# Empty places of the sorted edge tables: gathered as row 0, or left out of the gather by a bound

## The chip, the cores and the metric

One Trainium2 chip, one of its cores. The time is the device time of one execution in microseconds. The kernel before ran three times: 5455.31 us median, 5442.81 lowest, 5456.56 highest.

## The reference

A graph of 3125 nodes with 256 features goes through four residual layers, each behind a layer norm. Two of the four hold the attention over edges that this case is about:

```python
x = x + L0_gnn(...)   # sum over 50000 edges of weight * (x @ W)[src], into dst
x = x + L0_ffn(...)   # 32768 edges + one loop per node: attention with 16 features, 4 heads;
                      # it gives gates over 4 experts, then the experts
x = x + L1_gnn(...)   # three layers of _gat_conv over 50000 edges + one loop per node
x = x + L1_ffn(...)   # routing to 2 of 8 experts

def _gat_conv(x, src, dst, W, a_src, a_dst, b, n_nodes):      # 4 heads x 64 features
    h = (x @ W).reshape(n_nodes, Hh, Cc)
    e = leaky_relu(e_src[src] + e_dst[dst], 0.2)
    m = segment_max(e, dst); ex = exp(e - m[dst])
    alpha = ex / (segment_sum(ex, dst)[dst] + 1e-16)
    out = segment_sum(h[src] * alpha[:, :, None], dst)
    return out.reshape(n_nodes, Hh * Cc) + b
```

The sources of the edges are drawn evenly over the nodes. The targets of the 50000 edges crowd at the low nodes (3125 * u^2 for an even u). The outputs are the 3125 x 256 features.

## The kernel before

The program is a row of stages. A stage is one block in which every engine runs its own list of instructions, with semaphores between them; between two stages all engines meet at a barrier (L1709). There is no planner: the order on an engine is the order in which the code is written.

**Sorting.** The edges are sorted by target once, on the chip. A sorted table has columns of 128 places, one place per partition. Targets are grouped in buckets of 32 nodes, and a bucket starts a column of its own, so its last column is filled up with empty places; whole columns behind the last bucket are empty too, up to a multiple of 24. The table of the 50000 edges has room for 504 columns (`NCF`), that of the 32768 edges for 360 (`NCFG`). `permute_edges` (L408) brings the records of the 50000-edge table to their places with matmuls on one-hot matrices; `sum_edges` (L747) does the same for the 32768-edge table beside its own work. Both end with a few VectorE instructions that unpack the result: `whole` >> 2 is the place's node in its bucket plus one (zero at an empty place), `lows` becomes a penalty that the attention subtracts, and `sources` (`rows` in `permute_edges`) is the row of the source node. At an empty place it is 0, so an empty place reads row 0, and the penalty takes it out of the sum.

**Attention.** `attend_edges` (L846) runs in four stages: once on the 32768-edge table with rows of 24 numbers (`table_gate`, 96 bytes), and three times on the 50000-edge table with rows of 264 numbers (`table_att`, 1056 bytes). A group is 4 columns (`QD`); a ring of 6 slots (`U`) holds gathered rows, and one trip of the loop goes once around the ring.

- GpSimd (POOL) issues four indirect DMAs for each group (L892), each for one column, 128 rows. Before them it waits for the indices (`staged`, copied by ScalarE in L993) and, from the second trip on, until the slot has been used (`summed`).
- For each group VectorE waits until the slot's four DMAs have landed (`landed`), and subtracts the penalty (L911). TensorE transposes (L1056), VectorE takes the maximum (L942) and the running maximum, ScalarE and VectorE form the weights (L1007, L932, L1017), TensorE transposes back (L1064), ScalarE copies (L1024), and TensorE multiplies weights and rows (L1072). VectorE adds them to the bucket (L926).
- On VectorE, L911 of group q+1 stands ahead of L942 of group q.

At the start of such a stage SyncE loads the attention terms and the self loops' rows (L878, L880), and VectorE clears and copies a few small tables (L966 to L973).

Of the kernel before, what the change touches and what calls it, by code (L numbers as in the profile page):

```python
# [5 lines left out]
P = 128  # L6
# [4 lines left out]
NT = (N + P - 1) // P  # L11
# [15 lines left out]
ABOVE = 65536.0  # L27
RANKS = 4

ALU = mybir.AluOpType  # L30
# [18 lines left out]
NCFG = columns_sorted(EG)  # L49
# [358 lines left out]
def permute_edges(nc, block, m, name, edges, nch, record, lows, rows):  # L408
# [10 lines left out]
    def _(dve):  # L419
# [13 lines left out]
        whole, part = m.work[:, 13200:13200 + ncol].bitcast(I32), m.work[:, 13200 + ncol:13200 + 2 * ncol].bitcast(I32)  # L433
        chain.next(nc.vector.tensor_copy(whole, ps[0]))
# [3 lines left out]
        chain.next(nc.vector.scalar_tensor_tensor(rows, part, 1024.0, ps[1], ALU.mult, ALU.add))  # L438
# [301 lines left out]
def sum_edges(nc, block, m, name, table, rec, index, bucket, bias_in, edges, nch, record, lows, sources):  # L740
# [24 lines left out]
    def _(dve):  # L765
# [18 lines left out]
        def unpack():  # L784
            chain = Chain(dve, steps)
            dve.wait_ge(moved, fc)
            whole, part = m.sums.whole[:, 0:nch].bitcast(I32), m.sums.part[:, 0:nch].bitcast(I32)
            chain.next(nc.vector.tensor_copy(whole, ps_moved[0]))
            nc.vector.tensor_scalar(part, whole, 3, None, ALU.bitwise_and)
            chain.next(nc.vector.tensor_scalar(whole, whole, 2, None, ALU.logical_shift_right))  # L790
            nc.vector.tensor_scalar(lows, whole, -1.0, -STEP, ALU.add, ALU.mult)
            chain.next(nc.vector.scalar_tensor_tensor(sources, part, 1024.0, ps_moved[1], ALU.mult, ALU.add))
# [54 lines left out]
def attend_edges(nc, block, m, name, width, table, at_dram, nch, lows, rows_in, bucket, own_hot, starts, trip_count):  # L847
# [8 lines left out]
    s_ = lambda n: m.sem(f"{name}_{n}")  # L856
    passed, staged, fenced, masked, turned, reduced, lifted, leaked, top, exped, shrunk, turned2, evacd, summed, taken, steps, acc_in, at_in, tabled, ready = (
# [26 lines left out]
    def _(pool):  # L884
        def gather(q, s, first=False):
            pool.wait_ge(staged, q + 1)
            pool.sem_inc(passed, 1)
            if not first:
                pool.wait_ge(summed, q + (1 - U))
                pool.sem_inc(passed, 1)  # L890
            for t in range(QD):
                nc.gpsimd.indirect_dma_start(  # L892
                    out=rows[s][:, t, :], out_offset=None, in_=table[:, 0:rw],
                    in_offset=bass.IndirectOffsetOnAxis(ap=f.index[s][:, t:t + 1], axis=0)).then_inc(landed[s], 16)
# [9 lines left out]
    def _(dve):  # L904
# [60 lines left out]

        nc.vector.memset(running[:, 0:1], 0.0)  # L966
# [594 lines left out]
def memory(nc, ctx):  # L1561
# [91 lines left out]
    f.whole, f.part = view(NCFG), view(NCFG)  # L1653
# [160 lines left out]
```

## Time and profile before

| | |
|---|---|
| median of three runs | 5455.31 us |
| profiled execution, from the first instruction to the last (its span) | 4248.4 us |
| median less span | 1206.9 us |
| columns gathered in the four attention stages | 288, 456, 456, 456 |
| POOL busy | 2415.2 us (57%) |
| DVE busy (VectorE) | 2892.6 us (68%) |
| ACT busy (ScalarE) | 2269.8 us (53%) |
| PE busy (TensorE) | 2975.2 us (70%) |
| rows read by POOL's queue | 245.97 MB, 23.0% of the DMA engines' span |

The trace holds one profiled execution. It gives the span and no time of that execution outside it; the timed runs are longer than the span by 1206.9 us, for which there are no rows. All times of instructions below count from the first instruction of the span. A busy POOL is one that builds the descriptors of a gather; the transfer itself is not in that time.

### The profile page before, as it was taken

To read this page: it belongs to the slowest core of one execution; us is meant where nothing else is said; L and a number is where in the kernel's file an instruction comes from. 1 tells how busy PE (TensorE), PEld (TensorE's weight loads), DVE (VectorE), ACT (ScalarE), POOL (GpSimd) and SP (SyncE) were. 2 spreads that over 40 slices of the span, in tenths; PEclk is the share of its full clock that TensorE was granted. 3 is DMA by queue.
4 is the path that set the end of the run, shared out by engine and by line. 5 is a ranking of instruction groups with operands and counts; after the bars stand their busy time and mean duration, and the time that the engine had idled before them with its cause. 6 is when DMAs were issued, how large, how long until landed. Compare 5 with 4: busy or idle time off the path is not lost. (4 is left out here: it accounts for less than half of the span.)

```text
span 4248.4 us, 90006 instructions
## 1 busy us (share of the span) xinstructions
PE 2975.2 (70%) x23535; PEld 1861.8 (44%) x23535; DVE 2892.6 (68%) x9698; ACT 2269.8 (53%) x7978; POOL 2415.2 (57%) x2556
## 2 busy tenths in 40 slices
PE   5488957776666649997676666577666677766188
PEld 4252223333333337775344444344443444444166
DVE  6769977777447772224687777588777588777715
ACT  2006933333257762112687774487776388777423
POOL 3777767777357750000777773577775477777010
PEclk8558989999655559998555556655555755555599
DMA  2000023333210010001644442544443534444000
GB/s 97 6 2 2 2 78 105 106 106 105 46 14 10 10 30 12 12 0 43 138 108 108 108 108 60 125 108 108 108 108 84 113 109 108 108 108 102 3 23 30
DMA packets 199883, 292.96 MB, mean 69 GB/s; under 512 B 110324, under 2 KB 139998, under 8 KB 199678
## 3 DMA queue, kind: packets, MB, share of 16 engines
q0 software_dynamic: 108400, 245.97, 23.0%
q1 hardware_dynamic: 91310, 44.97, 4.4%
q8 instruction: 74, 1.21, 0.1%
q14 instruction: 99, 0.81, 0.1%
HBM read 270.29 MB, written 20.48 MB: 68 GB/s over the span
## 5 line engine op out<-in xcount | busy, mean ns | idle before, releaser
L892 POOL DMA_INDIRECT work<-table_att,work x1368 | 1297.2, 948 | 917.7 <-ACT work L993 500.7
L1064 PE MATMUL psum<-ident,work 128*128 128x128 f32 x1656 | 558.8, 474 | 362.1 <-ACT work L1017 362.1
L1017 ACT ACTIVATE work<-work 128x128 f32<-128x128 f32 x1656 | 529.6, 390 | 236.3 <-DVE work L932 236.3
L1072 PE MATMUL psum<-work 128*32 128x65 f32 (+1 forms) x13248 | 418.4, 294 | 314.1 <-ACT work L1024 261.8
L1064 PEld LDWEIGHTS psum<-ident,work 128*128 128x128 f32 x1656 | 301.3, 182 | 663.2 <-ACT work L1017 489.5
L1072 PEld LDWEIGHTS psum<-work 128*32 128x32 f32 x13248 | 331.3, 164 | 433.7 <-DVE acc L926 369.7
L932 DVE SCALAR_TENSOR_TENSOR work<-psum,work 128x128 f32<-128x128 f32 x1656 | 465.0, 343 | 82.2 <-ACT work L1007 77.3
L1007 ACT ACTIVATE work<-psum,work 128x128 f32<-128x128 f32 x1656 | 475.2, 375 | 49.7 <-DVE work L942 48.9
L926 DVE SCALAR_TENSOR_TENSOR acc<-acc,work,psum 128x65 f32 (+1 forms) x1656 | 445.5, 269 | 77.3 <-DMA acc<-table_att 16.6
L1056 PE MATMUL psum<-ident,work 128*128 128x128 f32 x1656 | 461.9, 435 | 36.2 <-DVE work L911 35.1
L474 POOL DMA_INDIRECT sorted<-xt x392 | 388.4, 991 | 171.3 <-issue 119.6
L817 POOL DMA_INDIRECT work<-table_sum,index x415 | 399.9, 964 | 142.0 <-PE psum L842 96.6
L911 DVE TENSOR_TENSOR work<-work,psum 128x512 f32<-128x512 f32 x414 | 283.8, 685 | 275.0 <-issue 168.3
L842 PE MATMUL psum<-work 128*128 128x256 f32 x830 | 289.0, 436 | 178.7 <-DMA work<-table_sum,index 107.0
L1000 ACT ACTIVATE psum<-iota,lows 128x32 f32<-128x32 f32 x1656 | 393.4, 311 | 31.3 <-DVE work L973 31.3
L892 POOL DMA_INDIRECT work<-table_gate,work x288 | 272.4, 946 | 181.8 <-ACT work L993 94.3
L1024 ACT COPY work<-psum 128x512 f32<-128x512 f32 x414 | 243.0, 587 | 198.6 <-PE psum L1064 198.6
L1056 PEld LDWEIGHTS psum<-ident,work 128*128 128x128 f32 x1656 | 296.3, 217 | 103.2 <-issue 59.4
L1414 PE MATMUL psum<-xt,work 128*128 (+1 forms) x960 | 267.8, 437 | 53.6 <-DMA work<-in_L_ffn_b_dram,expert_rows 35.3
L826 ACT ACTIVATE work<-work,xn 128x128 f16<-128x128 f16 x256 | 102.8, 401 | 358.1 <-DVE work L782 358.0
L942 DVE TENSOR_REDUCE work<-psum 128x512 f32 (+1 forms) x414 | 285.5, 690 | 3.1 <-issue 0.3
L1455 ACT ACTIVATE work<-psum,work 128x640 f32<-128x640 f32 x120 | 95.3, 794 | 342.6 <-PE psum L1414 342.5
(310 smaller groups left out, 4592.9 us busy)
## 6 DMA issues: line engine op xcount, KB each, us to landing
work<-table_att,work POOLq DMA_INDIRECT x1368
table_att<-acc SPq DMA_DIRECT2D x75, 132.0 KB
acc<-table_att SPq DMA_DIRECT2D x12, 812.5 KB
work<-table_sum,index POOLq DMA_INDIRECT x415, 2.7
sorted<-xt POOLq DMA_INDIRECT x392, 2.1
work<-table_gate,work POOLq DMA_INDIRECT x288, 2.3
work<-in_L_ffn_W_dram SPq DMA_DIRECT2D x8, 512.0 KB, 4.8
table_sum<-acc SPq DMA_DIRECT2D x25, 128.0 KB
```

Source lines behind the costliest of these rows:

```text
L474: nc.gpsimd.indirect_dma_start(out=rec_dram[s], out_offset=bass.IndirectOffsetOnAxis(ap=row[:, f:f + 1], axis=0), in_=record[:, f, :], in_ ...
L817: nc.gpsimd.indirect_dma_start(out=f.rows[c % RS][:, :], out_offset=None, in_=table, in_offset=bass.IndirectOffsetOnAxis(ap=index[:, c:c + ...
L842: nc.tensor.matmul(ps[c % PS], f.hot[c % PS][:, :], f.rows[c % RS][:, :], start=True, stop=True).then_inc(summed, 1)
L892: nc.gpsimd.indirect_dma_start(out=rows[s][:, t, :], out_offset=None, in_=table[:, 0:rw], in_offset=bass.IndirectOffsetOnAxis(ap=f.index[s ...
L926: nc.vector.scalar_tensor_tensor(acc[:, b, :], acc[:, b, :], f.fac[s][:, t:t + 1], ps_s[s % 2][:, t, :], ALU.mult, ALU.add).then_inc(taken, 1)
L932: ins = nc.vector.scalar_tensor_tensor(fifth, ps_z[s % 2][:, t * P:(t + 1) * P], dst[:, bass.ds(q * QD + t, 1)], fifth, ALU.add, ALU.max)
L1000: ins = nc.scalar.activation(ps_pen[s % 2][:, t, :], m.iota[:, 0:DB], ACT.Square, scale=STEP, bias=lows[:, bass.ds(q * QD + t, 1)])
L1007: ins = nc.scalar.activation(f.y[s % 2][:, t, :], ps_z[s % 2][:, t * P:(t + 1) * P], ACT.Identity, scale=0.2, bias=fifth_dst[:, bass.ds(q ...
L1017: nc.scalar.activation(f.pt[s % 2][:, t, :], f.y[s % 2][:, t, :], ACT.Exp, bias=f.neg[s][:, t, 1:2]).then_inc(exped, 1)
L1056: ins = nc.tensor.transpose(ps_z[s % 2][:, t * P:(t + 1) * P], f.z[s % 2][:, t, :, :].rearrange("p h d -> p (h d)"), m.ident[:, :])
L1064: nc.tensor.transpose(ps_p[s % 2][:, t * P:(t + 1) * P], f.pt[s % 2][:, t, :], m.ident[:, :]).then_inc(turned2, 1)
L1072: ins = nc.tensor.matmul(ps_s[s % 2][DB * h:DB * (h + 1), t, :], f.p[s % 2][:, t, DB * h:DB * (h + 1)], rows[s][:, t, h * w1:(h + 1) * w1] ...
```

## The change

At an empty place `sources` becomes 65536 + 0 in place of 0 (`NOWHERE`), worked out by two more VectorE instructions in each of the two unpackings. The gathers of the attention get a bound, the last row of the table (3199), and rows beyond it are left out without an error: nothing is written to their place in the slot. Since a place in a slot could then hold anything at first, VectorE sets the six slots to zero at the start of each attention stage, and the first gather into a slot waits for that (`cleared`). The gathers of `sum_edges` (L817) and the scatters of the sort (L474) are as before.

```diff
--- before.py
+++ after.py
@@ -25,6 +25,7 @@
 LN_EPS = 1e-5
 BIG = 1e30
 ABOVE = 65536.0
+NOWHERE = 65536.0
 RANKS = 4
 
 ALU = mybir.AluOpType
@@ -431,11 +432,14 @@
                                     ALU.is_equal, ALU.mult).then_inc(built, 1)
         dve.wait_ge(moved, fc)
         whole, part = m.work[:, 13200:13200 + ncol].bitcast(I32), m.work[:, 13200 + ncol:13200 + 2 * ncol].bitcast(I32)
+        nowhere = m.work[:, 13200 + 2 * ncol:13200 + 3 * ncol]
         chain.next(nc.vector.tensor_copy(whole, ps[0]))
         nc.vector.tensor_scalar(part, whole, 3, None, ALU.bitwise_and)
         chain.next(nc.vector.tensor_scalar(whole, whole, 2, None, ALU.logical_shift_right))
         nc.vector.tensor_scalar(lows, whole, -1.0, -STEP, ALU.add, ALU.mult)
-        chain.next(nc.vector.scalar_tensor_tensor(rows, part, 1024.0, ps[1], ALU.mult, ALU.add))
+        chain.next(nc.vector.tensor_scalar(nowhere, whole, 0.0, NOWHERE, ALU.is_equal, ALU.mult))
+        chain.next(nc.vector.scalar_tensor_tensor(nowhere, part, 1024.0, nowhere, ALU.mult, ALU.add))
+        chain.next(nc.vector.tensor_tensor(rows, nowhere, ps[1], ALU.add))
 
     @block.scalar
     def _(act):
@@ -789,7 +793,10 @@
             nc.vector.tensor_scalar(part, whole, 3, None, ALU.bitwise_and)
             chain.next(nc.vector.tensor_scalar(whole, whole, 2, None, ALU.logical_shift_right))
             nc.vector.tensor_scalar(lows, whole, -1.0, -STEP, ALU.add, ALU.mult)
-            chain.next(nc.vector.scalar_tensor_tensor(sources, part, 1024.0, ps_moved[1], ALU.mult, ALU.add))
+            nowhere = m.sums.nowhere[:, 0:nch]
+            chain.next(nc.vector.tensor_scalar(nowhere, whole, 0.0, NOWHERE, ALU.is_equal, ALU.mult))
+            chain.next(nc.vector.scalar_tensor_tensor(nowhere, part, 1024.0, nowhere, ALU.mult, ALU.add))
+            chain.next(nc.vector.tensor_tensor(sources, nowhere, ps_moved[1], ALU.add))
 
         for c in range(PS):
             mark(c)
@@ -854,6 +861,7 @@
     rw = hw + HEADS
     U = GROUP // QD
     s_ = lambda n: m.sem(f"{name}_{n}")
+    cleared = m.sem(f"{name}_cleared")
     passed, staged, fenced, masked, turned, reduced, lifted, leaked, top, exped, shrunk, turned2, evacd, summed, taken, steps, acc_in, at_in, tabled, ready = (
         s_(n) for n in ("passed", "staged", "fenced", "masked", "turned", "reduced", "lifted", "leaked", "top", "exped", "shrunk", "turned2", "evacd", "summed", "taken", "steps",
                         "accin", "atin", "tabled", "ready"))
@@ -885,13 +893,16 @@
         def gather(q, s, first=False):
             pool.wait_ge(staged, q + 1)
             pool.sem_inc(passed, 1)
-            if not first:
+            if first:
+                pool.wait_ge(cleared, s + 1)
+            else:
                 pool.wait_ge(summed, q + (1 - U))
                 pool.sem_inc(passed, 1)
             for t in range(QD):
                 nc.gpsimd.indirect_dma_start(
                     out=rows[s][:, t, :], out_offset=None, in_=table[:, 0:rw],
-                    in_offset=bass.IndirectOffsetOnAxis(ap=f.index[s][:, t:t + 1], axis=0)).then_inc(landed[s], 16)
+                    in_offset=bass.IndirectOffsetOnAxis(ap=f.index[s][:, t:t + 1], axis=0),
+                    bounds_check=NT * P - 1, oob_is_err=False).then_inc(landed[s], 16)
 
         trips = pool.value_load(trip_count, min_val=least, max_val=most)
         for k in range(U):
@@ -963,6 +974,8 @@
             nc.vector.tensor_tensor(f.drop[k], neg[:, :, 1], neg[:, :, 0], ALU.subtract).then_inc(top, 1)
             leak(q, k)
 
+        for s in range(U):
+            nc.vector.memset(rows[s], 0.0).then_inc(cleared, 1)
         nc.vector.memset(running[:, 0:1], 0.0)
         odd = reset.rearrange("p (c k) -> p c k", k=2)
         nc.vector.memset(odd[:, :, 1], 0.0)
@@ -1650,7 +1663,7 @@
     f = m.sums = Memory()
     f.rows = [view(D) for _ in range(16)]
     f.hot = [view(P) for _ in range(6)]
-    f.whole, f.part = view(NCFG), view(NCFG)
+    f.whole, f.part, f.nowhere = view(NCFG), view(NCFG), view(NCFG)
     assert at[0] <= WORK, at[0]
     at[0] = 0
     f = m.flash = Memory()
```

On VectorE, in the unpacking of the 50000-edge table (`permute_edges`; `sources` is what the diff calls `rows`), before:

```order
L434 CAST work<-psum 128x504
L435 TENSOR_SCALAR work<-work 128x504
L436 TENSOR_SCALAR work<-work 128x504
L437 TENSOR_SCALAR lows<-work 128x504
L438 SCALAR_TENSOR_TENSOR sources<-work,psum 128x504
```

and now:

```order
L436 CAST work<-psum 128x504
L437 TENSOR_SCALAR work<-work 128x504
L438 TENSOR_SCALAR work<-work 128x504
L439 TENSOR_SCALAR lows<-work 128x504
L440 TENSOR_SCALAR work<-work 128x504
L441 SCALAR_TENSOR_TENSOR work<-work 128x504
L442 TENSOR_TENSOR sources<-work,psum 128x504
```

The one instruction that formed `sources` has become three; the next one on the engine is the first of `merge_edges`. The unpacking in `sum_edges` grows in the same way, with 360 columns.

On VectorE, at the start of an attention stage with rows of 264 numbers, before:

```order
L966 MEMSET work 128x1
L968 MEMSET work 128x504
L969 COPY work<-starts 128x504
L971 COPY work<-psum 128x504
L972 COPY work<-psum 128x504
```

and now:

```order
L978 MEMSET work 128x1056 x6
L979 MEMSET work 128x1
L981 MEMSET work 128x504
L982 COPY work<-starts 128x504
L984 COPY work<-psum 128x504
L985 COPY work<-psum 128x504
```

Six clearings of 128 x 1056 numbers stand ahead of the stage's first instruction; in the stage with rows of 24 numbers they are 128 x 4 x 24 each. Nothing else is moved, and POOL issues the same instructions in the same order, 4 gathers for a group.

## Rows read from the trace of the kernel before

**Rows 1.** The page, its first line.

```profile
span 4248.4 us, 90006 instructions
```

**Rows 2.** Windows, gate attention stage and first of the three others; last PEclk, DMA, GB/s.

```profile
1198.50:1558.40 359.90, 212.32 (x2771) 138.29 (x2772) 260.99 (x973) 275.69 (x1047) 272.37 (x288) 0.50 0.12 11
2015.70:2586.70 571.00, 391.45 (x4416) 256.56 (x4416) 439.38 (x1552) 438.04 (x1671) 432.30 (x456) 0.50 0.46 114
```

**Rows 3.** L892, first of the three: ns min/median/max, first and last start.

```profile
L892 POOL DMA_INDIRECT work<-table_att,work x456: 945/949/958, 2015.7 to 2585.7; - x152
```

**Rows 4.** Timeline within that stage: start, us, engine, line, [idle <-releaser].

```profile
2403.86 0.69 DVE L942 TENSOR_REDUCE work<-psum 128x512 f32 x1
...
2405.38 0.95 POOL L892 DMA_INDIRECT work<-table_att,work  x1 [0.30 <-issue]
...
2408.22 0.69 DVE L911 TENSOR_TENSOR work<-work,psum 128x512 f32<-128x512 f32 x1 [0.81 <-issue]
...
2408.86 0.69 DVE L942 TENSOR_REDUCE work<-psum 128x512 f32 x1
```

**Rows 5.** Timeline, DVE, early in the third stage.

```profile
3444.08 0.68 DVE L942 TENSOR_REDUCE work<-psum 128x512 f32 x1
...
3448.83 0.68 DVE L942 TENSOR_REDUCE work<-psum 128x512 f32 x1
```

**Rows 6.** Timeline, end of the first of the three stages.

```profile
2585.73 0.95 POOL L892 DMA_INDIRECT work<-table_att,work  x1 [0.30 <-issue]
...
2592.49 0.69 DVE L911 TENSOR_TENSOR work<-work,psum 128x512 f32<-128x512 f32 x1 [2.41 <-issue]
...
2596.95 0.68 DVE L942 TENSOR_REDUCE work<-psum 128x512 f32 x1
```

**Rows 7.** Timeline, ends of the other two and of the gate stage.

```profile
3260.04 0.95 POOL L892 DMA_INDIRECT work<-table_att,work  x1 [0.30 <-issue]
...
3266.75 0.69 DVE L911 TENSOR_TENSOR work<-work,psum 128x512 f32<-128x512 f32 x1 [2.31 <-issue]
...
3921.25 0.95 POOL L892 DMA_INDIRECT work<-table_att,work  x1 [0.30 <-issue]
...
3928.31 0.69 DVE L911 TENSOR_TENSOR work<-work,psum 128x512 f32<-128x512 f32 x1 [2.72 <-issue]
...
1557.47 0.95 POOL L892 DMA_INDIRECT work<-table_gate,work  x1 [0.30 <-issue]
...
1560.80 0.69 DVE L911 TENSOR_TENSOR work<-work,psum 128x512 f32<-128x512 f32 x1 [1.48 <-issue]
```

**Rows 8.** DMA queues, 2300 to 2320 us: packets, MB, share of 16 engines.

```profile
q0 software_dynamic: 771, 2.16, 39.6%
```

**Rows 9.** DMA queues, 2575 to 2590 us.

```profile
q0 software_dynamic: 456, 1.31, 76.6%
```

**Rows 10.** Timeline, start of the first of the three stages.

```profile
2014.40 0.67 ACT L993 COPY work<-sources 128x4 int32<-128x4 int32 x6 [5.29 <-PEq L1709]
...
2014.60 0.48 DVE L968 MEMSET work<- 128x504 f32 x1
...
2015.71 0.95 POOL L892 DMA_INDIRECT work<-table_att,work  x1 [457.29 <-ACT work L993]
...
2026.70 0.69 DVE L911 TENSOR_TENSOR work<-work,psum 128x512 f32<-128x512 f32 x1 [3.54 <-DMA work<-table_att,work]
...
2031.70 0.68 DVE L942 TENSOR_REDUCE work<-psum 128x4 f32<-128x512 f32 x1
```

**Rows 11.** Timeline, DVE, unpacking in permute_edges and what follows.

```profile
556.84 0.67 DVE L438 SCALAR_TENSOR_TENSOR sources<-work,psum 128x504 int32<-128x504 int32 x1
571.61 1.46 DVE L498 TENSOR_TENSOR work<-work 128x1245 f32<-128x1245 f32 x1 [14.10 <-DMA work<-sorted]
```

**Rows 12.** Groups of instructions, DVE, x in sum_edges: busy, mean ns, idle before.

```profile
L775 DVE TENSOR_TENSOR x<-x,psum 128x256 f32 x415 | 174.3, 420 | 127.7 <-PE psum L842 123.0 <-DVE x L797 0.8 <-DVE sources L792 0.6
```

**Rows 13.** L474, the scatters of the sort: duration ns min/median/max.

```profile
L474 POOL DMA_INDIRECT sorted<-xt x392: 955/962/3138, 53.3 to 561.4; - x196
```

## The prediction

> **What bounds the kernel now.** I read the page first: the span is 4248.4 us [rows 1], while the timed median is 5455.3. The 1206.9 us between them have no rows. I take them as the same before and after, so the sum is made against the span and its result is carried over to the median microsecond for microsecond.
>
> Next the windows of the four attention stages. The reader is to see POOL's count: 288 gathers in 359.9 us, 456 in 571.0 us [rows 2], so 1.25 us each. POOL's busy share is 76%, but the rest is no slack: one gather takes 949 ns, between 945 and 958 over all 456 [rows 3], and 0.30 us of issue stands before each [rows 4]. POOL never stops for anything else, so the stage is as long as POOL's list: 456 x 1.25 = 571 us. The other two stages with 1056-byte rows also have 456 gathers; together 3 x 571 + 360 = 2073 us of the span go by POOL's issue rate.
>
> The timeline shows the distance of the second limit. In the middle of a stage two maxima (L942, one for each group) start 5.00 us apart, four gathers of 1.25 [rows 4]. Early in a stage, where the engines still work off what POOL had fetched ahead, they start 4.75 us apart [rows 5]: that is the compute chain's own pace, only 0.25 us under POOL's. The 0.50 of PEclk in those windows [rows 2] is the 1.2 GHz level, after stretches in which PE was busy 60 to 70% of the time. It is in the 4.75 already.
>
> The third thing is what lies behind the last gather. In the middle, L911 starts 2.84 us after its group's fourth gather started [rows 4]. For the last group of a stage that is 6.76 us [rows 6], 6.71 and 7.06 in the other two [rows 7], and 3.33 in the gate stage with its 96-byte rows [rows 7]. The last columns are empty, and all 128 rows of such a gather are row 0. The DMA rows say the same: 2.16 MB took 39.6% of 20 us [rows 8], 1.31 MB near the end took 76.6% of 15 us [rows 9]. Per MB that is 3.7 against 8.8 us of the queue. Many reads of one row are slow here; in the middle this hides behind POOL, at the end it does not.
>
> **The change part by part.**
>
> *Rows left out.* The 50000-edge table has 456 x 128 = 58368 gathered places, 8368 of them empty (14.3%). The gate table has 36864, with 4096 empty (11.1%). Those rows are no longer transferred. In the middle this is worth nothing: the transfers use 40% of the queue and POOL sets the pace. At the ends the lags should come back to the 2.84 us of the middle: 6.76 - 2.84 = 3.9, then 3.9 and 4.2, together 12.0 us. In the gate stage 0.5 us may go; I count nothing. Behind L911 comes a chain of fixed work, which moves with it: the group before it could start its maximum no sooner than 4.75 us after the one before, and the middle's spacing leaves that room.
>
> *The bound itself, on POOL.* No row shows a gather with a bound. POOL issues as many instructions as before, so the question is only whether 949 ns stays. Its price is multiplied by 1656 and nothing hides it, since POOL is the bound. From below: if all of a gather's time belonged to its rows, 14.3% fewer of them would take 136 ns off. From above: if each row were gone through twice, once for the bound, 949 ns would come on top. The nearest row for a gather's sister with other addressing is the scatter, 962 ns against 949 [rows 13, 3], so 13 ns apart, 22 us over all. The durations do not move with bytes either, so I take zero, and keep both ends for the rivals.
>
> *The clearing.* Six memsets of 1056 numbers at the start of a stage. One of 504 numbers takes 0.48 us [rows 10], so 1.0 us each, 6.0 us in all (six of 0.1 us in the gate stage). VectorE has room for more than half of it in the 3.54 us that it waited for the first landing before L911 [rows 10]. The rest fits into the 12.1 us from its first instructions at 2014.6 to L911 at 2026.70, which hold six instructions on 504 numbers or fewer, some 0.5 us each by the memset's row. The new wait on POOL stands ahead of the first gather of each slot, and the whole ring is queued behind it. The first slot is clear about 1.0 us into the stage, at 2015.5; POOL started at 2015.71 [rows 10]. The other slots come 5 us apart and are clear long before. If POOL needs after this semaphore what it needed after ScalarE's copy (2014.5 to 2015.7), its start moves by 1 us; if not, by nothing. Half of it, three times: +1.5 us. If the cover were gone altogether, it would be 3 x 6 = 18 us.
>
> *Two more instructions in each unpacking.* At most 0.67 us each for 504 numbers [rows 11]. In the first, VectorE then waits 14.10 us for a DMA [rows 11]: hidden. In `sum_edges` VectorE waits for TensorE 123 us in all before its additions [rows 12]; the 0.9 us there are made up over the last twelve columns: zero.
>
> *Sum.* -12.0 + 1.5 = -10.5 us. On the span 4248.4 - 10.5 = 4237.9, on the median 5455.3 - 10.5 = 5444.8.
>
> By the Trainium skill (DMA: Bandwidth & Descriptors, Anatomy of one DMA — SWDGE (gpsimd) path) a software DMA takes 2.0 us plus its bytes over 436 GB/s, whichever rows it reads; the lag at the end would then have another cause and would stay, and the sum would be +1.5 us, 5456.8. The trace speaks against that rule here, since gathers of equal size lag 2.84 and 6.76 us; this is the last rival below.
>
> **The rivals.**
>
> *POOL gets faster.* Fewer rows may mean less work for POOL. For it speaks that 949 ns for 128 rows is 7.4 ns a row, which looks like work by row; against it that the duration never varies, so that nothing shows a share by row. With 136 ns less, four gathers take 4 x 1.118 = 4.47 us, under the compute chain's 4.75. Then compute is the bound: from the first L942 at 2031.70 [rows 10], 113 steps of 4.75 end at 2568.5, where the last L942 was at 2596.95 [rows 6], 28.5 us less. The gate stage has 71 steps of 0.25, 17.8 us. Together 3 x 28.5 + 17.8 = 103, less some 5 us a stage, an estimate from the slow first landings (the 3.54 us wait), plus the 1.5: -87 us, 5368. The end effect is in it. The share needed by row is small: 63 ns less already reach 4.75.
>
> The Trainium skill (the same page, SWDGE vs HWDGE vs iDMA) has a Q7 core compute one descriptor pair for each DMA operation, which would make POOL's time go by the rows that are left, and give this rival's 5368. No row here shows a gather with fewer than 128 rows.
>
> *The bound costs POOL time (the other side).* The place is L892, each of its 1656 gathers. The price is any time for comparing and leaving out, paid in full because POOL never rests in these stages; from 6 ns a gather on (10.5 us / 1656) the change is no gain, from 16 ns on it is slower by over 0.3%. For it speaks that a row's 7.4 ns leave little room for a branch; against it the 13 ns between gather and scatter, which already differ in what is addressed. A tenth of a row's time more, 0.74 ns x 128 = 95 ns, makes 157 us: 5455.3 - 10.5 + 157 = 5602. A second pass would be 1572 us, which I hold very unlikely.
>
> *The ends do not shorten.* The bound may be applied without taking the load away, for instance if left-out rows still go through the queue, or the lag is that of the ring's last entries and not of row 0. Then only the clearing is left: +1.5 us, 5457. Against it speaks the queue's time per MB [rows 8, 9].
>
> **How the numbers follow.** Forecast (POOL unchanged, ends shorter) 0.47; POOL faster 0.14; the bound costs 0.33; ends unchanged 0.06. The predicted time is that of the forecast, 5445, with a range of its own of 5435 to 5457. The whole range runs from the faster rival, 5365, into the dear one as far as a price of 142 ns a gather (+235 us), 5680; beyond it I leave about 0.12, and below 0.03. A change of 0.3% is 16.4 us, about what a measurement of this kernel tells from none. The forecast's -10.5 lies inside it, but its parts can reach beyond: 0.16 of its 0.47 go to faster, 0.31 to the same. With the others: faster 0.14 + 0.16 = 0.30; same 0.31 + 0.06 and 0.02 for a bound of a few ns = 0.39; slower 0.31.
>
> **What would show it.** The first number to read is the mean of the attention gathers on POOL: 949 ns if right; under 900 the first rival, over 960 the second. L942 should stay 5.00 us apart in the middle; at 4.75 compute has become the bound. The lag from the last group's fourth gather to L911 should be under 3.2 us in all three stages. The queue's time per MB should be the same at the end as in the middle. POOL's first gather of a stage should start within 1 us of where it did. L498 should still wait about 13 us for its DMA. The prediction is wrong if the gathers' duration or their 0.30 us spacing has moved, or if the median moves and the span does not, since the 1206.9 us were only assumed to stay.

## The result: 0.6 to 0.8% slower, in a kernel with two paces

The changed kernel took 5485.42 us (median of 4 runs, 5474.84 to 5497.84) against 5455.73 (4 runs): 1.0063 times as long, 95% interval 1.0047 to 1.0079. The forecast was 5445 (5435 to 5457): the wrong direction, outside the forecast's own range and inside the whole one of 5365 to 5680. Ratios leave out one run, a 5813.08 us of e13 below, at a granted clock of 0.549 where its eleven others had 0.617 to 0.626. The profiled execution took 5474.84 us, and its page begins:

```profile
span 5473.1 us, 91690 instructions
```

Span and time agree here, unlike [rows 1], where 4248.4 us stood for a kernel timed at 5455. A profile of the unchanged kernel taken beside timed runs (experiment e1) explains it:

```profile
span 5446.1 us, 90006 instructions
```

The trace that the prediction read was of an execution unlike the timed ones. In five later series the same unchanged kernel took 5448, 4243, 5486, 5447 and 4246 us; the first two were on one and the same chip. I call this the quick and the slow pace; the instructions are the same in both, and nothing here shows what switches it. Its mark is in the second stage, where POOL issues scatters back to back beside the projection. The copies of the projection's tiles (L628) follow each other at 1.08 us in the quick trace:

```profile
85.98 0.37 ACT L628 COPY work<-psum 128x256 f32<-128x256 f32 x1 [0.71 <-PE psum L643]
87.07 0.37 ACT L628 COPY work<-psum 128x256 f32<-128x256 f32 x1 [0.71 <-PE psum L643]
```

and at 16.8 us in e1, where the second of these copies starts 13.9 us after TensorE's last transposes (L643) ended:

```profile
218.06 0.37 ACT L628 COPY work<-psum 128x256 f32<-128x256 f32 x1 [16.44 <-remote]
...
220.35 0.63 PE L643 MATMUL psum<-ident,xn 128*128 128x128 f32 x2
...
234.85 0.37 ACT L628 COPY work<-psum 128x256 f32<-128x256 f32 x1 [16.42 <-remote]
```

In the slow pace TensorE's signals are held back while POOL issues indirect DMAs. Work beside which POOL issues none is as fast in both paces: the copies of the projection ahead of the gate attention run from 1129.3 to 1190.3 us in the quick trace and from 1660.3 to 1721.3 in e1, 61.0 us in both. The stages with indirect DMAs lose 1.2 ms together. TensorE itself is not slower there: in the first wide attention stage (rows of 264 numbers) the granted clock is 0.50, the 1.2 GHz level, in both traces, and one of its transposes back (L1064) takes 476 ns in both. An attention stage in e1 looks like this (before, slow pace):

```profile
3022.71 0.69 DVE L942 TENSOR_REDUCE work<-psum 128x512 f32 x1 [2.43 <-remote]
3023.28 0.94 POOL L892 DMA_INDIRECT work<-table_att,work  x1 [1.87 <-remote]
...
3026.84 1.35 PE L1064 MATMUL psum<-ident,work 128*128 128x128 f32 x4 [1.26 <-ACT work L1017]
3027.03 0.95 POOL L892 DMA_INDIRECT work<-table_att,work  x1 [0.30 <-issue]
3029.33 0.69 DVE L942 TENSOR_REDUCE work<-psum 128x512 f32 x1 [2.47 <-remote]
```

Groups are 6.62 us apart, not the 5.00 of [rows 4], and POOL, which "never stops" in the quick trace, waits 1.9 us ahead of a group. L942 waits until 3029.33 for the transposes of L1056, whose last had ended at 3025.57. The trace's semaphore events tell that it is the signals that are late: six of TensorE arrive between 3029.11 and 3029.31, those of L1072 and L1056, whose last matmuls had ended 4.6 and 3.6 us before (the profile models matmul ends), and all four of L1064, and one of POOL's own between them, at 3029.16. In the quick trace the four of L1064 come 0.3 us apart. Now the changed kernel in the same place:

```profile
3022.95 0.69 DVE L953 TENSOR_REDUCE work<-psum 128x512 f32 x1 [5.00 <-DMA att<-in_L_ffn_att_dst_dram]
...
3023.59 1.00 POOL L902 DMA_INDIRECT work<-table_att,work  x1 [2.19 <-remote]
...
3026.46 0.67 DVE L922 TENSOR_TENSOR work<-work,psum 128x512 f32<-128x512 f32 x1
3027.11 1.35 PE L1077 MATMUL psum<-ident,work 128*128 128x128 f32 x4 [1.30 <-ACT work L1030]
3027.50 1.00 POOL L902 DMA_INDIRECT work<-table_att,work  x1 [0.30 <-issue]
...
3029.67 0.69 DVE L953 TENSOR_REDUCE work<-psum 128x512 f32 x1 [2.54 <-DMA att<-in_L_ffn_att_dst_dram]
```

The group is 6.72 us; the median of all is 6.70 against 6.61 (L911, L942 and L892 are now L922, L953 and L902). The load that the profile names ahead of L953 was done over a millisecond before; L953 waits for the same signal as L942 above. What answers to [rows 3] is the gather's own time, with a second row that before does not have:

```profile
L902 POOLq MOVE  x1656: 29/29/38, 1722.0 to 5135.3; - x184
L902 POOL DMA_INDIRECT work<-table_att,work x1368: 992/998/1218, 2666.0 to 5138.4; - x196
```

A gather with a bound takes 998 ns instead of 949, and POOL's queue moves the bound's value into a register ahead of each (29 ns). The page's DMA row, after and then e1:

```profile
q0 software_dynamic: 108400, 219.18, 15.5%
```

```profile
q0 software_dynamic: 108400, 245.97, 18.3%
```

27 MB fewer, but not one packet fewer. A gather makes 32 packets of four rows (4224 bytes) and 16 small ones; where rows are left out, the sizes in the trace are 3172, 2120, 1068 and 16 bytes, so a row left out leaves 4 bytes in a packet that is still there.

The end of the first wide stage, after, answers to [rows 6]:

```profile
3424.00 1.00 POOL L902 DMA_INDIRECT work<-table_att,work  x1 [0.31 <-issue]
...
3434.34 0.68 DVE L922 TENSOR_TENSOR work<-work,psum 128x512 f32<-128x512 f32 x1
```

and e1 in the same place:

```profile
3411.46 0.95 POOL L892 DMA_INDIRECT work<-table_att,work  x1 [0.30 <-issue]
...
3421.98 0.68 DVE L911 TENSOR_TENSOR work<-work,psum 128x512 f32<-128x512 f32 x1
```

10.3 us against 10.5, with nothing of DMA in the idle time: in the slow pace L911 of the last two groups still lies ahead when the last gather starts, the rows have landed before their turn, and nothing can be won there. The queue did become faster at the end, as forecast. From 3400 to 3430 us, after and then e1:

```profile
q0 software_dynamic: 768, 0.83, 11.1%
```

```profile
q0 software_dynamic: 426, 1.19, 33.7%
```

That is 4.0 us of the queue per MB against 8.5, where [rows 8] gave 3.7 for the middle. Packets of 4224 bytes that start between 3410 and 3420 us in the changed kernel, with four real rows each, take 0.17 us (median); e1's behind 3412 us, with row 0 four times, take 0.75. So row 0 is the cause of the slow end, not the place in the ring.

The start answers to [rows 10]:

```profile
2664.04 0.67 ACT L1006 COPY work<-sources 128x4 int32<-128x4 int32 x6 [5.29 <-PEq L1722]
...
2664.32 0.94 DVE L978 MEMSET work<- 128x1056 f32 x1 [4.26 <-PEq L1722]
...
2666.05 0.99 POOL L902 DMA_INDIRECT work<-table_att,work  x1 [467.25 <-DVE work L978]
```

Memsets of 0.94 us, and POOL's first gather 2.01 us after ScalarE's copies instead of 1.31.

### The profile page after: what moved, and what is told of

Same layout as the page of the kernel before. It is cut to its first block and busy times, and to the rows that moved or that the text cites. A ratio compares the mean times of both kernels' runs of the same rounds, so it can differ in the third digit from the quotient of the medians.

```text
span 5473.1 us, 91690 instructions
## 1 busy us (share of the span) xinstructions
PE 3002.8 (55%) x23535; PEld 1936.2 (35%) x23535; DVE 2848.4 (52%) x9726; ACT 2294.2 (42%) x7978; POOL 2512.4 (46%) x2556
## 3 DMA queue, kind: packets, MB, share of 16 engines
q0 software_dynamic: 108400, 219.18, 15.5%
## 5 line engine op out<-in xcount | busy, mean ns | idle before, releaser
L902 POOL DMA_INDIRECT work<-table_att,work x1368 | 1364.7, 998 | 1420.8 <-remote 567.4
L953 DVE TENSOR_REDUCE work<-psum 128x512 f32 (+1 forms) x414 | 285.9, 691 | 1019.5 <-DMA att<-in_L_ffn_att_dst_dram 835.5
L478 POOL DMA_INDIRECT sorted<-xt x392 | 402.2, 1026 | 169.8 <-issue 119.5
L902 POOL DMA_INDIRECT work<-table_gate,work x288 | 286.8, 996 | 288.9 <-remote 116.0
L670 PE MATMUL psum<-work 128*128 128x260 f32 (+1 forms) x400 | 140.5, 482 | 302.5 <-issue 203.6
L922 DVE TENSOR_TENSOR work<-work,psum 128x512 f32<-128x512 f32 x414 | 280.2, 677 | 50.2 <-DMA work<-table_att,work 24.4
L779 DVE TENSOR_TENSOR x<-x,psum 128x256 f32 x415 | 173.4, 418 | 237.3 <-PE psum L849 144.1
```

The source lines that it names most:

```text
L478: nc.gpsimd.indirect_dma_start(out=rec_dram[s], out_offset=bass.IndirectOffsetOnAxis(ap=row[:, f:f + 1], axis=0), in_=record[:, f, :], in_ ...
L902: nc.gpsimd.indirect_dma_start(out=rows[s][:, t, :], out_offset=None, in_=table[:, 0:rw], in_offset=bass.IndirectOffsetOnAxis(ap=f.index[s ...
```

## The experiments

Times are medians, ratios are against the unchanged kernel on the same chip, with 95% intervals. Which pace a series would meet couldn't be chosen.

### The change in its parts (e1 to e4, slow pace, before at 5447.9 us)

e1 is the kernel before. e2 has the bound alone:

```diff
-                    in_offset=bass.IndirectOffsetOnAxis(ap=f.index[s][:, t:t + 1], axis=0)).then_inc(landed[s], 16)
+                    in_offset=bass.IndirectOffsetOnAxis(ap=f.index[s][:, t:t + 1], axis=0),
+                    bounds_check=NT * P - 1, oob_is_err=False).then_inc(landed[s], 16)
```

e3 has everything but the bound (`NOWHERE = 0.0`, no `bounds_check`), and e4 is the changed kernel.

> The kernel before, unchanged, profiled once more. The trace read for the prediction has a span of 4248 us where the timed runs take 5455; the changed kernel's span (5473 us) and its time (5475 us) agree. Theory 1 (held signals, whatever the kernel): in the timed executions of both kernels TensorE's semaphore signals are held back while POOL issues gathers without a pause; the span here is then about 5454 us, with maxima (in the attention loop) some 6.5 us apart (4 gathers of 1.25 and 1.5 us of pause) in place of 5.0, and gathers of 949 ns. Theory 2 (the change brought the held signals): the span here is 4250 us again, maxima 5.0 us apart, and 1200 us still lie outside it.

> Only the bound on the attention gathers; empty places still read row 0, no clearing, so no row is left out. Theory 1 (the bound has a price on POOL, whatever it leaves out): the gathers take 998 ns in place of 949, and the time is +30 to +83 us (1656 x 0.05). Theory 2 (the price lies in leaving rows out, or in the clearing): gathers of 949 ns, 0 +- 5 us.

> Only the clearing of the six slots with the wait of the first gathers, and the three instructions of each unpacking with the added row number set to 0; no bound, empty places read row 0. Theory 1 (the bound is the price): gathers of 949 ns, +1 to +4 us for a later first gather. Theory 2 (the clearing costs, since POOL's queue stands behind it at four stage starts): +10 to +30 us.

> The changed kernel unchanged, timed in the same rounds as its parts. Theory 1: +30 us (5485), the sum of a price of the bound (+83 at most) and a gain of the rows left out (about -50). Theory 2 (the first measurement was a matter of the chip): within 0.3% of before.

Measured: e1 5448.97 (1.0002); e2 5477.21 us (1.0055, 1.0042 to 1.0069); e3 5454.08 (1.0011, 1.0002 to 1.0020); e4 5484.56 (1.0071, 1.0057 to 1.0084). The parts, 29.3 + 6.2 = 35.5 us, make the whole, 36.7: the bound costs, and the rows left out are worth nothing (e4's expectation had given them 50 us). Clearing moves the four attention stages of e3 by about 1 us in all; the rest of its 6 us (1 to 11 by the interval) lies mostly in the second stage, which took 965 to 984 us over thirteen slow profiles of all these kernels. Gathers are 998 ns in e2, where no row is left out, as in e4, where 14% are.

### Quick pace (e5 to e8, before at 4242.6 us)

e5 lets every place of the attention tables point beyond the bound (`ALU.is_equal` to `ALU.is_ge` in both unpackings), and so leaves out rows that the result needs. e6 has no bound but a memset behind each fourth gather:

```diff
+            if not isinstance(q, int) or q:
+                pool.wait_ge(padded, q)
+                pool.sem_inc(passed, 1)
+            nc.gpsimd.memset(m.prod[:, 0, 0:P], 0.0).then_inc(padded, 1)
```

e7 has the bound where `t < 2` alone. e8 pauses the scatters of the second stage:

```diff
             if f >= COPIES:
                 pool.wait_ge(sent[s], 16 * (f // COPIES))
+            if f >= COPIES and s == 0:
+                pool.wait_ge(sent[COPIES - 1], 16 * (f // COPIES))
```

> Leaves out all rows that the attention stages gather: every place of their tables, not the empty ones alone, points beyond the bound, so that no row of 1056 bytes is brought in those stages. Theory 'the price of the bound is paid once per gather on POOL, whatever its rows': gathers still last 0.99 to 1.00 us each, a group of four still takes 6.66 to 6.72 us, and the whole is that of the changed kernel, 5472 to 5492 us. Rival 'the rows' bytes count': without 1656 times up to 135 KB the transfers are short, groups fall to 6.3 us or less and the whole to under 5440 us. Rival 'the price is paid for each place beyond the bound' (the empty places as they are now are few in the middle of a stage): gathers grow well over 1.0 us and the whole over 5500 us.

> No bound at all: the kernel before, with a memset of 128x128 on POOL behind the fourth gather of each group (0.205 us in the trace of before, and the few ns of the wait ahead of it), which is about what four bounds cost POOL (4 x 0.05 us). Theory 'the bound costs by making POOL's part of a group longer than the rest of the loop': the same +0.05 to +0.10 us per group as with the bound, 6.66 to 6.72 us, and 5470 to 5490 us in all. Rival 'the bound costs elsewhere (in the DMA rings or in what the descriptors do)': groups stay at 6.61 us and the whole within 5 us of before. Rival 'all POOL time is on the path': +0.2 us for each of 414 groups, +83 us, 5531 us.

> The bound on the first two gathers of each group of four alone, nothing left out. Theory 'POOL's part of a group has 0.13 to 0.18 us of room before it decides': the two bounded gathers add 0.10 us to POOL, all of it hidden, groups stay at 6.61 to 6.63 us, and the whole is 0 to 8 us over before. Rival 'the price is in proportion': half of the 29 us of the full bound, +15 us, groups at 6.65 us. Rival 'the first bound in a group costs all': +29 us.

> The kernel before, with a pause of POOL in the second stage only: ahead of every fourth of the 392 scatters it waits until the scatter before has landed. Theory 'signals of TensorE are held back while POOL issues indirect DMAs back to back and pass when it pauses': the scatters end about 130 to 200 us later (near 720 us instead of 574), but the 25 tiles of the projection beside them come every 12 to 14 us or less instead of every 16.8 us, and what follows them runs beside the scatters; the stage, 972 us before, ends between 60 us earlier and 30 us later, and the attention stages stay as they are. Rival 'the projection is slow for another reason (the scatters' transfers, or TensorE's clock)': the tiles stay 16.8 us apart or follow the scatters' new rate by bytes, and the stage is later by the scatters' delay, 100 us or more.

Measured: e5 4319.84 (1.0186, 1.0172 to 1.0200), e6 4279.94 (1.0089, 1.0075 to 1.0103), e7 4306.91 (1.0154, 1.0141 to 1.0168), e8 4425.38 (1.0435, 1.0421 to 1.0449). The expectations were for the slow pace, so the misses say little of their theories, but here is the pace that the prediction had reasoned about. The changed kernel itself met the quick pace in no series; e5, which leaves out all rows, stands in for it. The page of e5 has

```profile
q0 software_dynamic: 108400, 58.37, 6.1%
```

the same packets with a quarter of the bytes, and gathers of 998 ns. The price is one for each gather with a bound, whatever it brings. In the middle of its first wide stage POOL has no pause, and a group is 5.22 us here (the median of all is 5.21, four gathers of 1.302):

```profile
2400.25 0.69 DVE L953 TENSOR_REDUCE work<-psum 128x512 f32 x1
...
2405.28 1.00 POOL L902 DMA_INDIRECT work<-table_att,work  x1 [0.30 <-issue]
2405.47 0.69 DVE L953 TENSOR_REDUCE work<-psum 128x512 f32 x1
```

and at its end, which answers to [rows 6]:

```profile
2626.77 1.00 POOL L902 DMA_INDIRECT work<-table_att,work  x1 [0.30 <-issue]
2629.02 0.69 DVE L922 TENSOR_TENSOR work<-work,psum 128x512 f32<-128x512 f32 x1 [0.78 <-issue]
```

2.25 us instead of 6.76; the other two stages have 2.21 and 3.04 instead of 6.71 and 7.06. The sum holds: 1656 gathers by 0.0495 us are +82 us, the three ends -13, together +69; the four attention stages of e5 are 70 us longer than in the trace of before. (The +77 of the medians is more because that trace's span is 6 us above this series' 4242.6.) In e6 each group grows by the 0.074 us that the memset delays POOL (414 x 0.074 = 31 us, measured 37 by the medians), in e7 by 0.137 (57 us, measured 64): in this pace any POOL time counts in full. In e8 the projection was not slow to begin with, and the pauses only put the scatters' end, and the stage with it, 179 us later.

### Slow pace again (e9 to e12, before at 5485.5 us)

The changed kernel, e2's, e6's and e5's once more.

> The changed kernel again, in whichever of two paces the chip is now (the kernel before took 5448 us in one series of runs and 4243 us in the next). In the slow pace: 5478 to 5490 us against 5448, +36 us, as twice seen. In the quick pace the four gathers of a group follow each other without a pause, and a group is POOL's own time: theory 'the bound costs 0.05 us on each of 1656 gathers and the ends of stages win back some 4 us each': groups at 5.19 to 5.21 us in the middle of a stage against 5.00, the last L911 work 7 us behind the last gather instead of 11, and +60 to +80 us in all, ratio 1.014 to 1.019. Rival 'the price is a fixed 30 us whatever the pace': ratio 1.007.

> The bound alone, nothing left out and nothing cleared. Slow pace: 5474 to 5484 us against 5448 (+29), as seen. Quick pace: all 1656 gathers longer by 0.05 us with no room beside them and no gain at the ends: +80 us, 1.018 to 1.020, 8 to 15 us more than the changed kernel. If leaving rows out is worth nothing in the quick pace either, it is as long as the changed kernel less the 2 us of the clearing.

> No bound: a memset of 128x128 behind the fourth gather of each group (it took 4280 us against 4243 in the quick pace: +0.08 us per group). Slow pace: if POOL's part of a group only begins to decide when it grows by 0.13 us, +0.08 us per group is hidden in it and the whole is within 5 us of before; if every addition counts by a third, as the bound's did, +10 to +14 us. Quick pace: +37 us again.

> Leaves out all rows that the attention stages gather. In the quick pace it took 4320 us against 4243, gathers 0.998 us each. Slow pace: if the price is one per gather on POOL whatever it brings, it is as long as the changed kernel, 5476 to 5492 us, with groups at 6.68 to 6.70 us; if the landings of rows have any part in the slow pace, groups fall under 6.6 us and the whole under 5450 us. Quick pace: 1.018 again, and within 10 us of the changed kernel.

Measured: e9 5527.61 (1.0079, 1.0064 to 1.0093), e10 5534.22 (1.0079, 1.0065 to 1.0094), e11 5490.28 (1.0007, 0.9997 to 1.0017), e12 5526.97 (1.0074, 1.0060 to 1.0087). All rows left out, some, or none: the same, so the transfers have no part in the slow pace. e11's memset, +0.08 us of POOL in each group, is hidden: POOL has room in the slow pace, and so the bound's price there is not simply POOL's time.

### The move and the check (e13 to e16, slow pace, before at 5446.9 us)

e13 is the changed kernel with the bound's value put into a register once a stage, e14 the changed kernel, e15 is e7's. e16 is e3 with two of the four gathers of a group left out, and so half of the rows that the result needs.

```diff
+        bound = pool.to_reg(NT * P - 1)
...
-                    bounds_check=NT * P - 1, oob_is_err=False).then_inc(landed[s], 16)
+                    bounds_check=bound, oob_is_err=False).then_inc(landed[s], 16)
```

> The changed kernel, but the bound's value is put in a register once a stage instead of ahead of each gather (a move of 29 ns on POOL's queue, 1656 times). Theory 'the move is most of the price': gathers back to 0.96 to 0.97 us, POOL's part of a group shorter by 0.12 us; slow pace: groups back within 0.03 us of before's and the whole within 10 us of before; quick pace: 48 us less than the changed kernel. Rival 'the check of the indices is the price': gathers stay at 0.997 us and the whole is that of the changed kernel within 5 us.

> The changed kernel once more, beside the others on the same chip. Slow pace: +36 to +43 us, as three times seen. Quick pace: +60 to +80 us, 1.014 to 1.019: 414 groups longer by 0.2 us, less what the ends of three stages win back, 4 us each.

> The bound on the first two gathers of each group, nothing left out. In the quick pace it cost 64 us, groups 0.13 us longer (1.007 us for a bounded gather, 0.959 for the next without). Slow pace: the room of 0.11 to 0.18 us per group hides nearly all of 0.13 us: 0 to +12 us. Rival 'in proportion': two thirds of the full bound's price, +24 to +30 us.

> Leaves out half of the attention rows: without a bound and with every place pointing into the table, but only the first two gathers of each group are issued. Slow pace: if TensorE's signals wait for POOL's burst, which now lasts 2.5 us instead of 5.0 and ends long before them, groups fall to between 4.8 and 6.0 us and the whole by 150 to 600 us; if the slow loop of signals has a length of its own, which the burst only fits into, groups stay at 6.6 us. Quick pace: POOL no longer decides, groups fall from 5.00 us to what DVE and TensorE need, 4.2 to 4.9 us, and the whole by 40 to 330 us.

Measured: e13 5454.75 (its eleven other runs 5453.13; 1.0012, 1.0000 to 1.0023), e14 5480.28 (1.0066, 1.0051 to 1.0081), e15 5478.69 (1.0063, 1.0048 to 1.0078), e16 4701.14 (0.8630, 0.8613 to 0.8646). First the gathers of e13, whose MOVE row is gone:

```profile
L902 POOL DMA_INDIRECT work<-table_att,work x1368: 992/998/1703, 2671.3 to 5118.3; - x196
```

The check itself makes a gather 50 ns longer, move or not: both of my theories had time and duration go together, and they do not. The whole gives back 25 to 27 of the change's 33.4 us though each gather is as long as in e14. The timelines show where. e13:

```profile
3003.33 0.69 DVE L954 TENSOR_REDUCE work<-psum 128x512 f32 x1 [2.44 <-DMA att<-in_L_ffn_att_dst_dram]
...
3003.90 0.99 POOL L902 DMA_INDIRECT work<-table_att,work  x1 [1.68 <-remote]
...
3009.97 0.69 DVE L954 TENSOR_REDUCE work<-psum 128x512 f32 x1 [2.50 <-DMA att<-in_L_ffn_att_dst_dram]
```

e14:

```profile
3005.86 0.69 DVE L953 TENSOR_REDUCE work<-psum 128x512 f32 x1 [2.50 <-DMA att<-in_L_ffn_att_dst_dram]
...
3006.49 1.00 POOL L902 DMA_INDIRECT work<-table_att,work  x1 [1.73 <-remote]
...
3012.54 0.69 DVE L953 TENSOR_REDUCE work<-psum 128x512 f32 x1 [2.54 <-DMA att<-in_L_ffn_att_dst_dram]
```

When TensorE's signals pass, L953 (L954 in e13) starts, and POOL's first gather 0.57 us later in e13, 0.63 in e14; these are the medians over the groups too, and before has 0.56. The groups are 6.62 and 6.69 us. e15, with half the moves and half the long gathers, has 0.63 and 6.68, as much as all; 0 to 12 us were expected of it and it took 32. The moves ahead of the later gathers don't show: from one gather's start to the next it is 1.30 us in e13 and in e14. So in the slow pace the price goes with the move ahead of the first gather of a group.

e16 was faster than even its first theory said (746 us instead of 150 to 600). Its groups are 4.75 us, the compute chain's own pace of [rows 5]. Its copies (L1036) start 0.04 us after TensorE's transposes, while a gather runs:

```profile
2824.18 1.35 PE L1076 MATMUL psum<-ident,work 128*128 128x128 f32 x4 [0.50 <-ACT work L1029]
...
2824.69 0.95 POOL L902 DMA_INDIRECT work<-table_att,work  x1 [0.30 <-issue]
...
2825.57 0.58 ACT L1036 COPY work<-psum 128x512 f32<-128x512 f32 x1 [0.47 <-PE psum L1076]
```

Four gathers in a row hold the signals back, two with 2.6 us of rest between do not. That refutes a slow loop with a length of its own; e12 shows that it is not the missing bytes. Whether all four gathers in two pairs with a rest between them would keep the 4.75 us was not run.

### How the price reaches the end (e17 and e18; the chip was in the quick pace, before at 4245.9 us)

e17 has the bound where `t == 0` alone. e18 has no bound, but e6's memset with 512 numbers a partition, ahead of the fourth gather.

> The bound on the first gather of each group alone. Its last gather then starts at about 0.63 + 1.31 + 1.26 + 1.26 = 4.47 us after the signals pass, where the room ends (4.46). Slow pace: theory A (POOL's part) gives groups of 6.61 to 6.63 us and +0 to +8 us, as with the bound in a register; theory B (the move itself) gives 6.68 to 6.69 us and +28 to +33 us, as with half of the bounds or all. Quick pace: POOL's part is the group, +0.06 to +0.08 us on each of 414, +25 to +35 us.

> No bound and no register move: a memset of 128x512 on POOL (about 0.5 us, of which some 0.3 to 0.4 us delay the gather behind it) between the third and the fourth gather of each group. Slow pace: theory A gives groups longer by the delay less the 0.14 us of room, 6.80 to 6.90 us, and +65 to +120 us; theory B gives 6.61 us and +0 to +8 us. Quick pace: the whole delay on each of 414 groups, +120 to +165 us.

Measured: e17 4270.56 (1.0061, 1.0047 to 1.0074), e18 4412.57 (1.0394, 1.0380 to 1.0408). Both came out as the quick pace asks: one bounded gather in four, 0.061 us later for the next, 414 x 0.061 = 25 us, measured 24.7; a delay of 0.396 us in e18, 414 x 0.396 = 164 us, measured 167. They can't tell theories A and B apart, which are of the slow pace. The slow traces can. In each of them the next maximum (L942, L953 or L954) starts a fixed time after the first gather of a group has started: 3023.28 to 3029.33 in e1 above, 3003.90 to 3009.97 in e13, 3006.49 to 3012.54 in e14. The medians are

| | first gather to fourth, us | first gather to the next signals, us | signals to the first gather, us |
|---|---|---|---|
| e1, e3 (no bound) | 3.76, 3.75 | 6.04, 6.04 | 0.56, 0.56 |
| e13 (bound in a register) | 3.90 | 6.05 | 0.57 |
| e15 (two of four bounded) | 3.88 | 6.05 | 0.63 |
| e2, e14 (four bounded) | 3.91, 3.91 | 6.06, 6.06 | 0.63, 0.63 |

The 0.15 us that the check adds behind the first gather change next to nothing: the signals are held until 6.04 to 6.06 us after its start in any case. What comes ahead of the first gather adds in full, since the next such stretch begins with it. Put beside e1 group by group, the first gathers of e14 start 30 us later behind their signals, summed up over 395 groups, and the groups are 27 us longer; in e13 it is 2 and -2. So theory B holds, and it is more than a correlation of medians: the 33 groups of e14 in which the first gather is 0.155 us later are 0.13 us longer, the 305 with 0.063 are 0.07 longer. (In e9 to e12 the fixed time is 6.13 to 6.16 us.) What ends the holding back, and why the first gather starts its time, stays open.

## Why the prediction was wrong

**The step that decided it: "The bound itself, on POOL ... I take zero".** It costs 0.049 us a gather, and a move of 29 ns ahead of it that the prediction did not count. The working beside it was right for the pace of its trace: multiplied by 1656 with nothing to hide it, from 16 ns on the kernel is slower by over 0.3%. With 49 ns it would have read -10.5 + 81 = +70 us, and e5, with all rows left out, has that in the quick pace (spans 4318.9 and 4248.4, +70.5; medians +77). The argument for zero was that 949 ns does not move with bytes and that the scatter is only 13 ns dearer; neither has a check in it. The rival "the bound costs POOL time" named the place and the mechanism; its size, 95 ns, was twice too large.

**The step behind it: the 1206.9 us "I take them as the same before and after".** They are not time outside the profile but the slow pace, and some 660 of them lie in the attention stages, which the change touches. POOL there is not the bound, and the price was 30 to 42 us, of which 25 to 27 of 33 go with the move (e13 against e14) and not with the 49 ns. So even the zero for the check would have been nearly right in the timed runs, by luck: the signals are held longer than the four gathers last. A span 22% under the timed median said that the trace showed another regime; I saw the number and argued it away.

**The ends, -12.0 us.** Right in mechanism and size in the quick pace (-13.0 in e5, with all rows left out), and nothing in the timed runs, where the last L911 comes 10.5 us after the last gather because the group before it has its own L911 still ahead, behind signals that come late. Many reads of row 0 are slow in both paces, as the queue's 8.8 and 8.5 us per MB show, and the changed kernel has 4.0. The rule of the Trainium skill that was weighed there (DMA: Bandwidth & Descriptors, Anatomy of one DMA — SWDGE (gpsimd) path) does not hold at these ends: by its figures 135 KB more would take 0.3 us longer, an estimate, and e5 and before differ by 4.5 (2.25 and 6.76 us). For e5's gathers, which bring next to nothing, the page of the profile has 2.1 us from issue to landing, and there its 2.0 us agree.

**The clearing, +1.5 us.** About 1 us in e3's attention stages: memsets of 0.94 us against 1.0 taken, and POOL's start 0.7 us later, between the 0 and 1 named.

**POOL gets faster.** Refuted by e5: with no row to bring a gather takes as long. The Trainium skill (DMA: Bandwidth & Descriptors, SWDGE vs HWDGE vs iDMA) has one descriptor pair computed for each DMA operation. The unchanged 108400 packets, with 4 bytes left of a row, agree with that if a row left out keeps its pair; the descriptors themselves no trace here shows.

**The ends do not shorten.** True of the timed runs, and the rival's reason "left-out rows still go through the queue" is true as well, as far as the packets stay, but the one is not the cause of the other: e5's ends do shorten. Its other reason, the ring's last entries, is refuted by the 0.17 us packets at the changed kernel's end.

No version here that brings all the rows beats the kernel before. Of those with a bound, e13 is the best in the slow pace (within 0.23% of before); in the quick pace its gathers would cost what e5's did, by their 998 ns, which was not run.

## What to carry to other kernels

Before you argue from a trace, hold its span against the timed runs; where they differ by more than a few per cent, get a profile of the timed regime, since which engine bounds a stage can be another there. Leaving work out by a test costs on every instruction that carries the test, so compare the test's price times all instructions with the work of those few that are left out. And put a constant that an instruction needs into a register once: ask what the queue does between the end of a wait and the first instruction behind it. Here 0.06 us in that place cost as much as the whole price, and 0.15 us behind it cost nothing.

## What the runs showed of the hardware

- A gather with a bound takes 998 ns against 949, with 0, 14 or 100% of its rows beyond it; its 48 packets stay, and a row beyond the bound leaves 4 bytes in its packet.
- One bound in four costs the gather that has it 62 ns (1.010 us in e17), all four 49 ns each.
- Gathers whose 128 rows are one and the same land late: L911 starts 6.7 to 7.1 us after them in the three ends of before, 2.2 to 3.0 with those rows left out (quick pace). A packet of four such rows took 0.75 us (e1), one of four different rows 0.2.
- One program on one core ran 28% longer in one series of runs than in another on the same chip (5447.9 and 4242.6 us). In the slow pace a signal of TensorE is seen up to 14 us late while POOL issues indirect DMAs at one in 1.3 us. Four of them in a row hold the signals until 6.04 to 6.16 us after the first has started; two of them and a rest of 2.6 us hold nothing back.
